# A fused attention and mixture-of-experts kernel: the clearing of a table, the routing, the token stores and one weight load change their places in the queues

## The reference, cut to what matters

```
x = x + tanh(g_attn) * attention(layernorm(x), ctx, ctx)      # 8 heads per batch, 16 channels each;
                                                              # the 512 columns are the positions
t = layernorm(x)                                              # 2048 tokens of 512 values
logits = t @ wg                                               # 8 experts
gate = max(softmax(logits)); expert = argmax(logits)          # one expert for each token
out = x + tanh(g_ffn) * gate * (t @ W[expert].T + b[expert])  # W is (8, 512, 512)
```

## Time and profile before

| | |
|---|---|
| median of 3 runs | 548.47 us (543.82 to 548.65) |
| the profiled execution, its own time | 546.76 us |
| its span on the core | 544.8 us, 1.96 us less than its time |
| PE busy | 497.7 us, 91% of the span |
| DVE, ACT, POOL busy | 435.4, 348.3, 344.2 us |
| SP's queue | not counted as busy; read from the timeline of its DMA issues |
| DMA | 92.96 MB, mean 171 GB/s |

### The profile page before, as it was taken

One profiled execution on the slowest core, in us unless ns is written; L12 is line 12 of the kernel. 1 busy time (PEld: TensorE's weight loads), 2 busy tenths in 40 slices (PEclk: granted clock), 3 DMA queues, 4 the chain that ended last, 5 costly groups with the idle time before them and its releaser, 6 DMA issues. The chain is left out here.

```text
span 544.8 us, 10088 instructions
## 1 busy us (share of the span) xinstructions
PE 497.7 (91%) x2580; PEld 177.3 (33%) x2580; DVE 435.4 (80%) x851; ACT 348.3 (64%) x428; POOL 344.2 (63%) x531
## 2 busy tenths in 40 slices
PE   0288999999999999999999999998999999899993
PEld 0012223333323233333323232333332245344451
DVE  5898889889889989899998999899988867334341
ACT  3224978888787988888887879896767842111110
POOL 7535367666776767767667778886456537554541
PEclk9999999999999999999999999999999999999998
DMA  4887356575767757675657667665544645644310
GB/s 131 226 185 232 100 169 175 147 234 140 225 193 183 214 171 198 198 224 171 198 170 208 193 172 214 181 180 166 155 130 139 216 162 186 198 144 133 104 60 0
DMA packets 51760, 92.96 MB, mean 171 GB/s; under 512 B 22898, under 2 KB 24946, under 8 KB 51688
## 3 DMA queue, kind: packets, MB, share of 16 engines
q1 hardware_dynamic: 36624, 67.33, 43.9%
q0 software_dynamic: 10560, 24.93, 14.0%
q10 hardware_dynamic: 4536, 0.23, 0.5%
HBM read 68.96 MB, written 28.41 MB: 179 GB/s over the span
## 5 line engine op out<-in xcount | busy, mean ns | idle before, releaser
L952 DVE TENSOR_REDUCE neg_max<-ps_ring 128x1 f32<-128x512 f32 x480 | 306.9, 681 | 26.1 <-PE ps_ring L1346 24.2
L853 ACT ACTIVATE probs<-ps_scores 128x1024 f32<-128x1024 f32 x256 | 251.2, 1022 | 60.7 <-PE ps_scores L1365 54.9
L1346 PE MATMUL ps_ring<-stacks 96*128 96x512 bf16 x480 | 166.8, 384 | 5.6 <-DVE neg_max L952 5.0
L1365 PE MATMUL ps_scores<-stacks 128*128 128x512 bf16 x512 | 153.6, 382 | 3.2 <-ACT probs L853 1.7
L1388 PE MATMUL ps_pv<-probs,v_ones 128*32 128x512 f32 x992 | 132.1, 604 | 0.9 <-DVE scale L992 0.9
L1346 PEld LDWEIGHTS ps_ring<-stacks 96*128 96x128 bf16 x480 | 46.4, 97 | 156.8 <-DVE neg_max L952 111.6
L1449 PE MATMUL ps_scores<-w_sb,f_xt 128*128 x184 | 83.3, 594 | 0.2
L1365 PEld LDWEIGHTS ps_scores<-stacks 128*128 128x128 bf16 x512 | 48.2, 100 | 55.0 <-ACT probs L853 15.1
L829 ACT COPY f_xt<-ps_scores 128x512 f32<-128x512 f32 x22 | 12.8, 584 | 69.4 <-PE ps_scores L1432 69.4
L1449 PEld LDWEIGHTS ps_scores<-w_sb,f_xt 128*128 128x128 f32 x184 | 33.0, 190 | 32.4 <-issue 32.1
L565 POOL TENSOR_TENSOR prep<-prep 128x512 f32<-128x512 f32 x30 | 34.7, 1159 | 13.5 <-ACT prep L800 13.5
(11 more groups left out here) (144 smaller groups left out, 492.3 us busy)
## 6 DMA issues: line engine op xcount, KB each, us to landing
stacks<-parts_dram SPq DMA_DIRECT2D x224, 64.0 KB, 3.1
parts_dram<-prep POOLq DMA_DIRECT2D x15, 768.0 KB
w_sb<-w_t SPq DMA_DIRECT2D x16, 512.0 KB
recs_dram<-rec SPq DMA_DIRECT2D x16, 512.0 KB
stacks<-parts_dram SPq DMA_DIRECT2D x32, 192.0 KB, 3.2
prep<-x_perm SPq DMA_DIRECT2D x16, 256.0 KB
prep<-k_perm SPq DMA_DIRECT2D x16, 256.0 KB
v_in<-v_t SPq DMA_DIRECT2D x16, 256.0 KB, 2.9
```

Of the source, the lines that this page charges most:

```text
L853: nc.scalar.activation(probs[:, k % 2, 2 * jp:2 * jp + 2], ps_scores[:, jp], ACT.Exp).then_inc(exp_done, 1)
L952: nc.vector.tensor_reduce(neg_max[:, g, j, c:c + 1], ps_ring[:, SLOT[tile]], AX.X, ALU.max, negate=True).then_inc(ring_free, 1)
L1346: nc.tensor.matmul(ps_ring[:, SLOT[tile]], q_stack[0:KS, into.p, g, j, c * 128:(c + 1) * 128], k_stack[0:KS, into.p, g, j], start=True, st ...
L1365: last = nc.tensor.matmul(ps_scores[:, jp, j % 2], k_stack[0:KA, B.p, g, j, c * 128:(c + 1) * 128], q_stack[0:KA, B.p, g, j], start=True, ...
```

## The change

The token table is cleared, and the first piece of the weights loaded, inside batch 0, after the fourth pair of scores. In every later batch that has one, `load_weight` stands behind `spread_recips` of the high inverses instead of ahead of it. Experts, places and gates are found two steps later on DVE, the gates' exponentials three steps later on ACT. On POOL, in batch 14, the four token stores of group 1 stand behind the shifts and behind the copy of the values, two and two; in batch 15 the token stores of group 2 stand between the second and the third gather. Behind the batches, POOL reads the slots of phase 1 ahead of the last `rstd2`, and tile 5 is gathered ahead of tile 1's scatter; DVE adds tile 0's bias after the last attention output and takes the columns of phase 1 after tile 0; PE transposes tile 7 behind all four chunks of tile 6.

```diff
@@ block.sync
             load_rows_keys(Batch(1, 1))
-            clear_table()
-            load_weight(Batch(0, 0))
...
                 if prev and by_transfer(B.plus(-1)):
                     store_recips(B.plus(-1), 1)
+                    spread_recips(B.plus(-1), 1)
                     load_weight(B)
-                    spread_recips(B.plus(-1), 1)
...
                 if B.known(0):
                     sp.wait_ge(dve_const, DVE_CONSTS)
+                    sp.wait_ge(scores_ready, 4)
+                    clear_table()
+                    load_weight(B)
                 if not isinstance(B.b, int) or B.b + 2 < NB:
                     load_stack(B.plus(2), 0)
@@ block.gpsimd
-            def end(B):
+            def last_batch(B):
...
-                for s in range(NREC):
+                for s in range(2):
                     gather(s)
                 number_places(2)
                 store_tokens(*GROUPS[2])
+                for s in range(2, NREC):
+                    gather(s)
...
-                if B.known(RANKED[1]):
-                    number_places(1)
-                    store_tokens(*GROUPS[1])
                 if prev:
                     add_low(B.plus(-1))
...
                     add_high(B.plus(-1))
                 split_maxima(B.plus(1), 0)
+                first, end = GROUPS[1]
+                if B.known(RANKED[1]):
+                    number_places(1)
+                    store_tokens(first, first + 2)
                 if prev:
                     rstd2(B.plus(-1))
                 if prep:
                     lows(B.plus(3))
                 copy_values(B.plus(1))
+                if B.known(RANKED[1]):
+                    store_tokens(first + 2, end)
...
             last = Batch(7, 1)
+            read_slots(1)
             rstd2(last)
-            read_slots(1)
             for s in range(NSLOT):
-                first = s + NREC in (PHASES[1][1], FIRST_LATE)
+                first = s + NREC == FIRST_LATE
@@ block.scalar
-                        if k == 2 and B.known(ROUTED[group]):
+                        if k == 5 and B.known(ROUTED[group]):
                             exp_gates(group)
@@ block.vector
-                            if B.known(ROUTED[group]) and at == (1, 1):
+                            if B.known(ROUTED[group]) and at == (3, 1):
                                 find_experts(group)
-                            if B.known(RANKED[group]) and at == (1, 1):
+                            if B.known(RANKED[group]) and at == (3, 1):
                                 find_places(group)
-                            if B.known(RANKED[group]) and at == (1, 3):
+                            if B.known(RANKED[group]) and at == (3, 3):
                                 find_gates(group)
...
             invert_sums(last, 1)
-            add_bias(0)
             take_logits(last.plus(-1))
             turn_back(last)
             add_attention(last)
+            add_bias(0)
             for s in range(NSLOT):
                 if s == 2:
...
-                    take_columns(1)
...
                 if s == 0:
                     name_experts(1)
                     take_tiles(1)
+                    take_columns(1)
@@ block.tensor, in expert and in the loop over tiles
                 last.then_inc(y_full, 1)
+                if NC in between:
+                    between[NC]()
...
-                    expert(s, {2: lambda: turn_next(s)})
+                    expert(s, {NC if s + 1 == FIRST_LATE else 2: lambda: turn_next(s)})
```

More of the change, by code:

```diff
@@ L722, in emit @@
                 if B.known(NB - 1):
-                    return end(B)
+                    return last_batch(B)
                 split_maxima(B, 1)
```

## The result

The changed kernel takes **567.09 us** (median of 6 runs, 559.12 to 572.2), the kernel before 548.56 beside it: ratio 1.0303 [1.0248, 1.0358], slower by 3%, outside the predicted range. The ratio leaves out the slower executions, of the changed kernel the two of 569 us and more. The profiled execution has a span of 563.2 us.

A forecast was written before the change was run, and what follows sets the result against it. The prediction took PE as the bound of a batch, with hardly any slack between SP's queue and PE. Terms -1.0 - 1.2 - 1.0 - 0.6 - 1.5 + 3.0 = -2.3 gave 546.2 us; range 540 to 551.5.

The forecast's parts named there:

- Weights behind the spread, 14 batches: SP's queue, batches 1 to 14: the uncovered weight issue lengthens SP's chain, 0.3 us each where SP lacks slack, +3.0 us.
- The sign that the prediction named: On SP, the interval from the store to the low shifts of the same batch grows by 0.5 to 0.6 us.
- SP sets the pace: Rival, chance 0.22: SP's chain outgrows PE's, 0.6 us a batch over eleven batches plus 0.5 once; 550.3 us.
- The rival of a faster store and spread: Rival, chance 0.18: without weights in flight the store's landing falls towards 0.65 us and `stats2` waits go; 539.8 us.
- Table and first weights: Batch 0: moving both issues behind the fourth pair of scores removes PE's wait for ACT, -1.0 us.
- Routing and token stores: Routing, batches 9, 10, 13, 14, avoids POOL's multiply, -1.2 us; batch 14's token stores behind the shifts, -1.0 us.
- third rival: Rival, chance 0.16: in batches 10 and 14 the routing meets POOL again, two meetings at 1.1 us; 548.4 us.
- Batch 15 and tail: Batch 15: biases leave earlier, shortening PE's wait for a shift, -0.6 us; tail: tile 7's first chunk begins earlier, -1.5 us.

The follow-up runs named there:

- experiment 1: The changed kernel with the weight load of batches 1 to 14 ahead of the spread of the high inverses again: 542.9 us, ratio 0.9896.
- experiment 7: The changed kernel with rows and keys issued in the wait between the low inverses' store and their spread: 549.89 us, ratio 0.9983.
- experiment 4: The changed kernel with the weight load split in halves, 64 partitions ahead of the spread and 64 behind it: 568.42 us, ratio 1.0349.
- experiment 9: The changed kernel with the weights issued in the wait of the low store instead of behind the high spread: 551.52 us, ratio 1.0002.
- experiment 10: The changed kernel with the weights of batches 1 to 14 issued by ACT behind its fifth exponential instead of by SP: 557.29 us, ratio 1.0118.
- experiment 14: The kernel of experiment 1 with the store of the records also issued in the high wait, behind the weights: 550.51 us, ratio 1.0019.
- experiment 2: The kernel before with only the weight load of batches 1 to 14 moved behind the spread: 575.76 us, ratio 1.0503.
- experiment 12: The kernel before with only the moved routing and token stores of batches 8 to 14: 549.29 us, ratio 0.9986.
- experiment 13: The kernel before with only the new order of batch 15 and of the tail: 548.37 us, ratio 0.997.
- experiment 11: The kernel before with only the clearing of the table and the first weights moved into batch 0: 547.01 us, ratio 0.9934.
- experiment 8: The kernel of experiment 1 with rows and keys also issued in the wait of the low store: 545.57 us, ratio 0.9899.

## Why the prediction was wrong, step by step

**The failed step** is "Weights behind the spread, 14 batches", +3.0. Its mechanism was seen: an issue loses its cover, SP's queue is full. Its size was not: 22 us (experiment 1). The prediction let SP's chain grow by the issue alone, 0.47 to 0.7 us a batch, and let half of that go into "the waits that SP still has", with the landings as they were. The runs show that the low store's landing grows most. From low store to low store, batch 7 takes 27.25 us instead of 24.35: 0.6 more for the uncovered issue, 0.8 for the stacks behind it, which take longer to issue, and 2.05 for the low store's landing, less 0.5 at other issues. The sign that the prediction named, the interval from the high store to the low shifts, grew by 1.4 us there, not by 0.5 to 0.6. The high store's landing stayed as it was, as the prediction had it. And SP had next to no waits left in batches 3 to 8 that could have taken half.

Why the landing grows: the 1.4 us put the low store behind POOL's 768 KB, and SP stands still until it has landed. The prediction followed SP's order alone and did not ask what another queue sends at that moment. The rows of all these kernels agree with it, and so does experiment 7, where 17.6 of the 22 us go when the low store moves ahead of rows and keys, and so ahead of POOL's store. It fits that 256 KB cost as much as 512: there too most low stores are behind POOL's (experiment 4). But no run moves POOL's store alone, so this link is read from the traces and not shown by an experiment of its own; and the 6 to 12 us that experiments 9, 10 and 14 lose, with none to three such stores, come about in other ways.

The rival "SP sets the pace" named the place and the side, and its price, 0.6 a batch, was a sixth of the 3.3 that batches 3 to 8 lost (19.5 / 6). (The 0.5 that it adds once comes to 0.33 by the rows it names: half of 293.09 - 290.74 - 1.7.) The rival of a faster store and spread had a true core, but the store's wait did not shorten, and 0.2 us is all that the spread wins: it lands in 2.0 us in experiment 1, and in the changed kernel (DMA issues of the stretch 190 to 290 us, columns as above) in 1.8:

```profile
scale<-recip_dram SPq DMA_DIRECT2D x28, 32.0 KB, 1.8
```

**Table and first weights**, -1.0: right in kind, -3.6 in size. The profile of before showed a small case, a wait of 1.00 us. PE's wait in batch 0 in three other executions with the table in front, experiments 2, 12 and 13 (ACT's, ahead of it, was 4.81, 5.04 and 3.67 us):

```profile
55.28 0.61 PE L1365 MATMUL ps_scores<-stacks 128*128 128x512 bf16 x2 [2.87 <-ACT probs L853]
```

```profile
55.75 1.03 PE L1368 MATMUL ps_scores<-stacks 128*128 128x512 bf16 x2 [3.09 <-ACT probs L856]
```

```profile
54.49 0.60 PE L1367 MATMUL ps_scores<-stacks 128*128 128x512 bf16 x2 [1.98 <-ACT probs L855]
```

After, the two issues stand at 47.77 and the wait is gone.

**Routing and token stores**, -1.2 and -1.0: the first came, batch 13 takes 25.02 instead of 26.09 us (25.2 in experiment 12, where SP is not late); the second did not, batch 14 takes 26.46 instead of 26.10. All of experiment 12 is -0.8 against the -2.2 of both terms, and not clear of nothing. POOL's low output of batch 14 starts 7.3 us into the batch instead of 14.4, but the gates now meet POOL's multiply. Batch 14 after:

```profile
427.11 1.26 POOL L598 TENSOR_TENSOR high_num<-high_num,scale 128x512 f32<-128x512 f32 x1 [4.07 <-DMA scale<-recip_dram]
427.20 1.21 DVE L1082 TENSOR_SCALAR entries<-gate_inv,gates 128x4 f32<-128x4 f32 x1
...
429.05 0.28 PE L1357 MATMUL ps_ring<-identity,neg_max 128*16 128x128 f32 x1 [1.40 <-DVE neg_max L958]
```

DVE's 0.23 us instruction takes 1.21 and ends with POOL's, and PE waits 1.40. That is the third rival's mechanism, here and in batch 9, where DVE's row of L1053 (L1047 before) takes 1.20 us instead of 0.23 beside a POOL row. The Trainium skill, "SBUF — State Buffer", section "SBUF: two separate sides", says that the lock on the shared ports is held for the whole instruction; the trace agrees in that the two rows end 0.04 us apart, though nothing here shows that this DVE instruction takes those ports. It hangs on SP's time: in experiment 1 the same instruction takes 0.23 us and batch 14 25.4.

**Batch 15 and tail**, -0.6 and -1.5: 1.5 us together by the windows, -1.7 by experiment 13. PE's wait for a shift in batch 15 is gone; between the tiles, against the earlier trace rows:

```profile
485.34 5.32 PE L1455 MATMUL ps_scores<-w_sb,f_xt 128*128 x12
...
491.39 0.63 PE L1438 MATMUL ps_scores<-identity,recs 128*128 128x128 f32 x4 [0.74 <-DMA recs<-recs_dram,token_cols]
492.06 0.58 ACT L835 COPY f_xt<-ps_scores 128x512 f32<-128x512 f32 x1 [5.93 <-PE ps_scores L1438]
...
492.89 1.98 PE L1455 MATMUL ps_scores<-w_sb,f_xt 128*128 x4 [0.87 <-ACT f_xt L835]
```

Tile 6 runs in one piece and PE waits 0.74 instead of 2.45 us for tile 7, as predicted. Without the weights the terms add to -5.3; experiment 1 measured -5.7. That is luck: by experiments 11 to 13 one term was 2.6 us too small and the others together 1.8 too large.

## What to carry to other kernels

An issuing queue has no busy share, so price a step moved in it by its slack in the stage it touches: how often and how long it waits there for producers rather than for its own transfers. If that slack is near zero, look at what the later entries of the queue will then meet in the other queues. Here 1.4 us of delay put an 8 KB store behind another queue's 768 KB, and a batch lost 3.3 us. A long wait for a store is not itself a loss (experiment 8). A wait in such a queue is a place for one issue, not for any number of bytes ahead of what the wait is for (experiment 14); and a stall that depends on transfers is sized from several executions, not from one.

## What the runs showed of the hardware

- A DMA of 127 rows in place of 128 made transfers behind it in the same queue land late, the values after 15.4 us instead of 2.9 and the spread after 8.3 instead of 2.0, and the kernel took 1.54 times as long.
- SP waited 1.1 us for an 8 KB store to land where it had stood idle for 1 us or more ahead of it (before, batches 0, 12 and 13), 1.9 to 2.4 in nine of batches 1 to 11 straight behind 512 KB of loads, and 3.2 to 5.0 in all 37 cases in which POOL had begun a 768 KB store 0.55 to 3 us earlier in its own queue. None of the 37 is set up by moving POOL's store alone.
